# A graph network on one Trainium2 core: the first one-hots of a round are made before the wait for the turned weights

## The reference, cut to what matters

```
e = leaky(a_src[src] + a_dst[dst], slope)
m = segment_max(e, dst);  ex = exp(e - m[dst])
s = segment_sum(ex, dst)
out = segment_sum((ex / s[dst])[:, :, None] * h[src], dst)
```

## Time and profile before

| what | value |
| --- | --- |
| three runs | 6548.13, 6557.96, 6566.23 us |
| profiled execution, span from first to last instruction | 6525.8 us |
| what lies around the span, against the median of the runs | 32.2 us |
| PE matmul busy | 4307.6 us, 66% of the span |
| DVE busy | 3511.9 us, 54% |
| ACT busy | 3189.4 us, 49% |
| POOL busy | 3265.5 us, 50% |
| gathers of the graph streams (L978) | 1758.9 us for 1856 of them and 865.7 us for 904 |
| ACT L1241 (spread, first part) | 2784 instructions, 880.9 us |
| ACT L1244 (spread, second part) | 696 instructions, 502.2 us |
| mean granted TensorE clock | 0.796 of full speed |

### The profile page before, as it was taken

How to read it: one execution, slowest core, us unless ns; L and a number is a source line. 1 busy time by engine, 2 the same in 40 slices (tenths; PEclk the granted TensorE clock), 3 DMA queues, 4 the chain that set the end, 5 groups by cost and what they waited for, 6 DMA issues and landing times.

```text
span 6525.8 us, 75215 instructions
## 1 busy us (share of the span) xinstructions
PE 4307.6 (66%) x17795; PEld 2999.8 (46%) x17795; DVE 3511.9 (54%) x10013; ACT 3189.4 (49%) x7093; POOL 3265.5 (50%) x3443
## 2 busy tenths in 40 slices
PE   2896565666653696677676766645555555589798
PEld 2554444444432584355555554434444444433455
DVE  4376565656566437566666666655554545552211
ACT  1365555555542223466666666545555555544222
POOL 0125666666655535355555555546666666501222
PEclk9997777767775798777877778777776677799999
DMA  3292444444431333233333333334444444310110
GB/s 101 63 281 79 122 122 122 121 122 121 123 100 54 103 110 113 80 105 103 105 100 106 101 102 102 96 109 114 113 114 115 113 115 112 97 65 23 33 36 26
DMA packets 347491, 659.78 MB, mean 101 GB/s; under 512 B 78834, under 2 KB 196608, under 8 KB 346664
## 3 DMA queue, kind: packets, MB, share of 16 engines
q0 software_dynamic: 156336, 433.43, 24.1%
q1 hardware_dynamic: 190732, 221.55, 11.6%
HBM read 540.63 MB, written 115.42 MB: 101 GB/s over the span
## 4 chain that ended last, share of the span: by engine, by line
PE 26%; ACT 14%; another core or an unknown queue 13%; issue 7%; DVE 6%; POOL 2%; DMA 0%; DVEq 0%; SPq 0%; POOLq 0%; ACTq 0%
PE ps L1194 6%; ACT AR L1241 4%; PE ps L2560 3%; PE ps L2541 3%; PE ps L2249 2%; ACT AR L1254 2%; ACT AR L1252 2%; ACT AR L1244 2%; PE ps L2046 1%; POOL D_sx L1635 1%; PE ps L1678 1%; PE ps L1669 1%; PE ps L2261 1%; DVE AR L1087 1%
## 5 line engine op out<-in xcount | busy, mean ns | idle before, releaser
L978 POOL DMA_INDIRECT AR<-D_z,SRCI x1856 | 1758.9, 948 | 1231.6 <-issue 490.6
L1194 PE MATMUL ps<-AR 128*128 128x264 f32 (+2 forms) x5568 | 1923.5, 504 | 280.5 <-issue 133.0
L1194 PEld LDWEIGHTS ps<-AR 128*128 128x128 f32 x5568 | 1345.4, 254 | 641.6 <-issue 181.6
L978 POOL DMA_INDIRECT AR<-D_h,SRCI x904 | 865.7, 958 | 458.1 <-issue 242.8
L1241 ACT ACTIVATE AR<-iota_n,NREL 128x128 f32<-128x128 f32 x2784 | 880.9, 389 | 205.4 <-remote 143.9
L1087 DVE TENSOR_TENSOR AR<-ps,AR 128x264 f32 (+2 forms) x1392 | 589.5, 424 | 544.9 <-remote 228.7
L1065 DVE TENSOR_TENSOR AR<-AR,ps 128x1024 f32<-128x1024 f32 x696 | 836.8, 1202 | 6.3 <-ACT AR L1267 6.0
L1244 ACT ACTIVATE AR<-AR,ones 128x512 f32<-128x512 f32 x696 | 502.2, 722 | 22.6
L1266 ACT ACTIVATE AR<-ps 128x128 f32<-128x128 f32 (+2 forms) x174 | 51.1, 294 | 864.9 <-remote 728.3
L1254 ACT ACTIVATE AR<-AR,ones 128x1024 bf16<-128x1024 bf16 x348 | 399.5, 1148 | 11.3
L1252 ACT ACTIVATE AR<-AR,iota_p 128x1024 bf16<-128x1024 bf16 x348 | 394.7, 1134 | 20.3 <-DMA AR<-D_rel 20.3
(11 more groups left out here) (437 smaller groups left out, 7814.2 us busy)
## 6 DMA issues: line engine op xcount, KB each, us to landing
AR<-D_rel SPq DMA_DIRECT2D x348, 256.0 KB
D_sx<-AR SPq DMA_DIRECT2D x8, 6370.0 KB
AR<-D_z,SRCI POOLq DMA_INDIRECT x1856
AR<-D_h,SRCI POOLq DMA_INDIRECT x928
D_y<-AR SPq DMA_DIRECT2D x106, 128.0 KB, 1.7
AR<-in_L_ffn_Wd SPq DMA_DIRECT2D x8, 1024.0 KB
AR<-D_mask SPq DMA_DIRECT2D x58, 128.0 KB
D_h<-AR SPq DMA_DIRECT2D x49, 132.0 KB
```

What stands on the lines that cost most here:

```text
L978: e.indirect_dma_start(out=GV[:, u % 48, :], out_offset=None, in_=D_row[L.i], in_offset=bass.IndirectOffsetOnAxis(ap=SRCI[:, u:u + 1], axi ...
L1194: t = e.matmul(banks[n % 3][:, 0:YW], Sr[:, u % 8, :], GV[:, u % 48, :], start=(i == 0), stop=(i == 1))
```

## The change

`spread(k, 0)`, the one-hots of the first quad of the round that is being prepared, was the last step of an iteration on ACT. It now stands inside `weights(k)`, behind the exponential and ahead of the wait for the turned weights (`al_ps`). Nothing is added or removed.

```diff
                 e.wait_ge(x_ready, K + 1)
                 e.activation(B2[0:P, :], B2[0:P, :], ACT.Exp).then_inc(ex_ready, 1)
+                spread(k, 0)
                 e.wait_ge(al_ps, K + 1)
                 e.activation(g_units(L, 16 * k, 16)[:, :, :, D], w[:, 0:P].rearrange("p (u h) -> p u h", h=H), ACT.Copy)
                 e.activation(RR[:, 0:H], w[:, 128:128 + H], ACT.Exp).then_inc(r_ready, 1)
...
                 if k < NG2:
                     weights(k)
                 side.after_weights(e, k)
-                if k < NG2:
-                    spread(k, 0)
```

## The result

The changed kernel takes 6595.12 us (median of 14 runs, 6571.54 to 6609.95) beside 6548.34 us for the kernel before (14 runs, 6510.41 to 6584.85): ratio 1.0068, 95% interval 1.0049 to 1.0087. It is slower by 0.7%, some 45 us, and the forecast was "no change, if anything a little faster".

The account below looks back on a forecast made before the run. POOL's gathers and stops were taken to bound streams 0 and 2, PE's chain stream 1; 0 of 21 us plus about 5 us gain gave 6520.8 us profiled, 6553 us with 32.2 us added; range 6508 to 6606.

Parts of the forecast that it names:

- The cover: Streams 0 and 2: DVE's other work and PE's quad(g, 3) hide the later copy; without it the price would be 46 us.
- the late copy: ACT's copy of the turned weights, 1.2 us later in 27 rounds of stream 2, 0.8 in 17 of stream 0; taken as nothing.
- 46.3 us or less: Sign: two rounds of streams 0 and 2 this short, with as many stops, would make the step on the release wrong.
- the gain at the quad: PE's first quad starts earlier without the spread ahead: 0.38 us in streams 0 and 2, 0.88 in stream 1; 44 us if all passed on.
- What is late next: What passes on to the time: 0 of 21 us in streams 0 and 2, about 5 us gain in stream 1.
- The 0.88 us: Stream 1: how much earlier each waiting first quad would start without spread, square and root ahead of it; 26 such waits.
- The 22.9 us: Stream 1: gain if every earlier first quad passed on whole, 26 x 0.88; a quarter was taken, about 5 us.
- slower: Rival: later copy in 44 short-wait rounds of streams 0 and 2 delays weighing; price 46 us, 6604 us; chance 0.15.
- fewer stops: Rival: POOL stops twice instead of three times per two rounds in streams 0 and 2; 130 us gain, 6428 us; chance 0.07.
- higher clock: Rival: first quads of stream 2 rise to PE's upper clock level; 71 us gain, 6487 us; chance 0.04.
- the gain passes on whole: Rival: all of PE's earlier first quads in the three streams shorten the time; 44 us, 6514 us; chance 0.17.
- by this rule: Step: a quad that starts earlier between two releases changes the next release by nothing; otherwise the whole gain would stand.

Follow-up runs that it names:

- e2: Kernel before, with the spread of the first quad ahead of the copy in streams 0 and 2 alone; 6555.25 us, ratio 1.0000.
- e6: Kernel before; in stream 1 a tiny copy announces the first quad's spread at the new place, ACT's similar work stays at the old, into idle memory; 6540.60 us, ratio 0.9956.
- e1: Kernel before, with the spread of the first quad ahead of the copy in stream 1 alone; 6601.26 us beside 6555.35, ratio 1.0068.
- e7: Kernel before; in stream 1 the last quad's spread stands behind the exponential instead of ahead of it; 6495.28 us, ratio 0.9912.
- e3: Kernel before; in stream 1 the first quad's spread stands behind the copy and small exponential, ahead of the side work; 6537.20 us, ratio 0.9984.
- e5: Kernel before; in stream 1 ACT does the first quad's spread at the new place but announces it at the old one; 6592.30 us beside 6553.36, ratio 1.0070.
- e14: The changed kernel itself, again, on a chip where the kernel before takes 5753.01 us; 5752.34 us, ratio 0.9993.
- e15: Kernel before; in stream 1 the first quad's spread is left out, a tiny copy announces it at the old place; 6549.69 us beside 6544.87, ratio 1.0012.
- e16: The kernel of e10 run again, on a chip of the first kind; 6556.02 us, ratio 1.0022.
- e4: Changed kernel; in stream 1 ACT's copy of the projection's input moved ahead of the second one-hot and last quad's spread; 6601.81 us, ratio 1.0072 to the kernel before.
- e8: e7 with the edit of e3 added, against the kernel before; 6473.57 us, ratio 0.9879.
- e17: Changed kernel; in stream 1 the copy of the third transposes moved behind the one-hot and last quad's spread; 5815.04 us beside 5758.58 of the kernel before, ratio 1.0094.
- e10: Kernel before; in stream 1 about 1.8 us of ACT work into idle memory added between exponential and copy, spread at its old place; 5755.23 us, ratio 1.0002.
- e12: Kernel before; in streams 0 and 2 POOL waits at every eighth gather until the one before has landed; 6471.81 us, ratio 1.1247.

## Why the prediction was wrong

**What held.** Streams 0 and 2: the quad follows DVE's weighing by 0.10 us, the copy comes late in the short rounds (it had no idle time before it in 28 rounds of each), neither moves the time, and e2's ratio is 1.0000. The cover that I had named for the late copy (DVE busy with scores, `quad(g, 3)` until after the weighing) held there. In stream 2 of the changed kernel DVE waited for `r_ready` ahead of a weighing 5 times, 4.2 us in all:

```profile
DVE AR L1065 <- ACT AR L1268: 4.2, 5, 1.1
```

POOL's stops in stream 2 are 199.8 us in 83 waits, against 198.3 in 90. (The sign "46.3 us or less" for two rounds could not decide: stream 2 took 46.0 us for two rounds on average before already, and 46.3 after.) That the gain at the quad is real, if small, held as well: e6 has it alone, 0.3 to 0.4%.

**What failed** is the sentence on stream 1 under "What is late next": the path "holds nothing of the spread; the quads behind it may help a little", priced at 5 us of gain with bounds of 0 and 22.9. Measured there: 0.68% or 45 us of loss (e1). The bound below was set at nothing because I looked at PE's waits only. In stream 1, unlike in 0 and 2, ACT is the late engine at the exponential (it waited for DVE there in 1 round of 55), and PE and ACT hand the attention's blocks to and fro within the round, across the hold-back. Where ACT's steps stand in that round moves the time both ways: by 45 us up in e1, by 58 us down in e7. The rows were in the trace before: the idle time ahead of L2067 and PE's wait for it. The prediction priced a late copy for streams 0 and 2 alone; for stream 1 that term was rightly nothing, since ACT's wait there covers the spread, so the loss is not that rival either.

The price of the gain in stream 1 was also misread. The 0.88 us come from the quad at 3211.80, but its row puts PE's idle time down to DVE's add, L1087. That add ended at 3211.79 and the spread (3211.03 + 0.72) at 3211.75, so by these rows an earlier spread alone would have gained nothing in that round:

```profile
3211.36 0.43 DVE L1087 TENSOR_TENSOR AR<-ps,AR 128x260 f32 x1 [0.21 <-DVE AR L1087]
```

The 22.9 us built on it had no ground, though e6's gain is of about that size.

**The rival "slower"** had a like price (46 us), but its place was streams 0 and 2 and its point of decision the cover there, which held. That the size came out is chance. The rivals "fewer stops" and "higher clock" did not happen; "the gain passes on whole" fits the announcement alone in stream 1 (e6) and nothing in streams 0 and 2.

**What stays open.** By what way ACT's 2 us become 45 us is not settled. Shown: the loss is made in stream 1 (e1, e2); it doesn't come from the early announcement (e6), nor from a late copy of the turned weights, which is late in 4 rounds; it needs the spread's work ahead of the copy (e3, e5); and it is absent on a chip on which PE's announcements aren't held back (e14). Not shown: whether ACT's being ahead or its work in the wait does it. e15 and e16, which were to tell, lost next to nothing, on a chip on which the changed kernel wasn't measured. Seen in the traces, and only argued: more of the hold-backs then meet the copy of the third transposes, where PE waits for ACT. Those waits of PE were 144.4 us in the changed kernel, 142.2 in e4, 113.3 in e5, 90.0 in e1, against 52.1 before, 29.9 in e7, and 37.3 in e8. But e2, whose stream 1 has the old order, had 104.9 us in its profiled execution, e3 and e6, which lose nothing, 71.9 and 83.9, and e15 and e16 80.5 and 86.0: single executions of one order scatter, so these numbers go with the time only roughly and prove no way. The kernel that would have tried it (e17) met only a chip on which it can't be seen.

## What to carry to other kernels

Before work is moved into an engine's wait, ask whether that engine is the late one elsewhere in the same round. Here a row said so, "ACT waited for its partner in 1 of 55 rounds", and what was worth moving stood ahead of the step that others wait for, not behind it: the same idea, applied to the last quad's spread instead of the first's, gained 0.9% where this change lost 0.7%, and 1.2% together with the first quad's spread behind the copy. Read in the trace whether an experiment does what it is named for: the "late copy" of e10 was late in few rounds. And run on more than one chip, with the changed kernel itself in each group: the loss of 0.7% was absent on the second kind.

## What the runs showed of the hardware that was not expected

Two kinds of chip. The kernel before took 6545 to 6555 us in three of the groups of runs, as in the first comparison, and 5753 to 5759 us in the other three, with no median between. The program and the bytes are the same, and the DMA engines' time for the queue that carries the gathers nearly so. Queue rows (packets, MB, share of 16 engines) of the kernel before and of e14:

```profile
q0 software_dynamic: 156336, 433.43, 24.1%
```

```profile
q0 software_dynamic: 156336, 433.43, 27.9%
```

24.1% of 6525.8 us are 1573 us, 27.9% of 5758.7 are 1607 us. What differs is when others hear of PE: on the first kind up to several microseconds after the record of the matmul (6.4 us at 3414.43), together with the end of the gathers under way as I read the earlier trace rows; on the second at once (the longest wait of ACT's copy for `back` in stream 1 of e14 is 1.0 us). In e14 no wait of ACT, DVE, PE or POOL in the graph streams has a "remote" row; in the kernel before ACT's copy of the turned weights alone has 100. The mean granted clock differs too, about 0.85 on the second kind and 0.80 on the first; what follows from what isn't shown. The prediction took a held-back announcement for a property of the kernel; by these runs it goes with the chip, or its state. Why, no run here tells. The rule of the Trainium skill that I had leaned on, DMA: Bandwidth & Descriptors, "Anatomy of one DMA — SWDGE (gpsimd) path", prices a transfer and says nothing of a tie between PE's announcements and its end, so the step "by this rule" in the prediction was mine and not the rule's. As a price my estimate of 2.3 us is near the stops of 2.2 to 2.8 us; where POOL waits for a landing itself, in e12, it stopped for 2.6 and for 4.0 to 4.1 us in turn, and the estimate fits only the shorter.
